# A fused decoder layer: new hand-written step orders for four engines, and a table of 281 identity products emptied

## What is computed

```python
def step(Sst, inp):                       # part 1: gated delta rule, 16 heads of 16
    qt, kt, vt, bt, gt = inp
    Sd = gt[..., None, None] * Sst
    kS = jnp.einsum('bhk,bhkv->bhv', kt, Sd)
    Snew = Sd + jnp.einsum('bhk,bhv->bhkv', kt, bt[..., None] * (vt - kS))
    ot = jnp.einsum('bhk,bhkv->bhv', qt, Snew)
    return (Snew, ot)
...
attn = a1 - lam * a2                      # part 2: two softmax attentions over 64 context tokens
...
ye = jax.nn.silu(jnp.einsum('bsd,eod->bseo', x1, expert_w) + expert_b)   # part 3: 8 experts,
combined = jnp.einsum('bse,bseo->bso', rw, ye)                           # two of them weighted per token
```

## Time and profile before

| | |
|---|---|
| median of 3 runs | 1671.31 us (1670.07 to 1680.73) |
| the profiled execution | 1671.47 us |
| its span | 1669.7 us |
| mean granted TensorE clock | 0.965 |
| TensorE, matmul busy | 1515.5 us, 91% of the span |
| VectorE busy | 1215.3 us, 73% |
| ScalarE busy | 858.9 us, 51% |
| GpSimd busy | 205.8 us, 12% |

### The profile page before, as it was taken

The page is one execution under the profiler, slowest core; times in us unless marked ns, Lnnn a source line. Parts: engine busy times, 40 slices in busy tenths (PEclk is TensorE's granted clock), DMA queues, the critical chain, the costliest instruction groups (busy, mean ns, idle before and its releaser), DMA issues.

```text
span 1669.7 us, 38572 instructions
## 1 busy us (share of the span) xinstructions
PE 1515.5 (91%) x16038; PEld 1013.4 (61%) x16090; DVE 1215.3 (73%) x3201; ACT 858.9 (51%) x1620; POOL 205.8 (12%) x212
## 2 busy tenths in 40 slices
...
DMA packets 20214, 31.69 MB, mean 19 GB/s; under 512 B 1480, under 2 KB 17864, under 8 KB 19784
## 3 DMA queue, kind: packets, MB, share of 16 engines
...
...
## 4 chain that ended last, share of the span: by engine, by line
PE 74%; DVE 17%; ACT 6%; issue 3%; DVEq 0%; ACTq 0%
PE bank L1766 11%; PE bank L1505 8%; PE bank L1714 7%; PE bank L1392 5%; PE four L1575 4%; PE bank L1704 4%; PE bank L1690 4%; PE bank L1507 3%; PE bank L1417 3%; DVE cs L1340 3%; PE four L1594 2%; PE four L1643 2%; PE bank L1432 2%; PE four L1417 2%; PE four L1627 2%
## 5 line engine op out<-in xcount | busy, mean ns | idle before, releaser
L1766 PE MATMUL bank<-w_sb,cs 128*128 128x512 f32 x512 | 260.2, 615 | 1.5 <-ACT cs L786 0.3
L786 ACT ACTIVATE cs<-bank 128x512 f32<-128x512 f32 x128 | 76.3, 596 | 235.0 <-remote 141.6
L505 POOL TENSOR_TENSOR decayed<-state,pk 128x512 f32<-128x512 f32 x64 | 70.7, 1105 | 825.1 <-DVE state L1160 825.1
L740 ACT COPY cs<-bank 128x512 f32<-128x512 f32 x128 | 74.9, 585 | 158.2 <-PE bank L1704 158.2
L1714 PE MATMUL bank<-vx_sb,cs 128*128 128x136 f32 x1024 | 141.3, 293 | 10.1 <-ACT cs L740 10.1
L1714 PEld LDWEIGHTS bank<-vx_sb,cs 128*128 128x128 f32 x1024 | 132.7, 199 | 22.3 <-ACT cs L740 14.6
L1505 PE MATMUL bank<-hT,w_sb 128*128 128x512 f32 x256 | 134.2, 649 | 9.9 <-ACT pre L590 6.8
L1766 PEld LDWEIGHTS bank<-w_sb,cs 128*128 128x128 f32 x512 | 90.0, 190 | 69.0 <-issue 60.1
L1340 DVE SCALAR_TENSOR_TENSOR cs<-cs,rwt 128x256 f32<-128x256 f32 x224 | 113.1, 505 | 24.7 <-ACT cs L786 13.0
L1704 PE MATMUL bank<-c_sb,cs 128*128 128x128 f32 x512 | 86.4, 294 | 30.7 <-ACT cs L740 16.1
L1238 DVE TENSOR_TENSOR cs<-bank,pkc 128x512 f32<-128x512 f32 x128 | 82.0, 682 | 30.6 <-PE bank L1704 30.6
...
## 6 DMA issues: line engine op xcount, KB each, us to landing
...
```

Of the source, the lines that this page charges most:

```text
L1766: mm(dst, x1T[:, k, b * TB:b * TB + TB], ew[:, k, ep * 512:ep * 512 + 512], start=k == 0, stop=False)
```

## The change

The lists of all four engines are replaced, the table KEEP is emptied, and `keep` (which then issues nothing) looks up another event to wait for. All steps stay, and each engine still runs each step once per turn. The core of the diff:

```diff
 ORDER = {
     "pe": steps('''
-        sum.0 sum.1 decay sum.2 +turn1.0 +turn1.1 -turn2.0 grow -turn2.1 -qx.0 sum.3 -sc.0.0 -qx.1 -sc.0.1 vturn raw.0
+        sum.0 sum.1 decay sum.2 +turn1.0 -turn2.0 +turn1.1 grow -turn2.1 -qx.0 sum.3 -sc.0.0 -qx.1 -sc.0.1 vturn raw.0
...
     "act": steps('''
...
-        -turn5.1 -turn6.0 -hnorm.1 -ffd.0 -turn6.1 osq.1 onorm.0 onorm.1 -ffd.1 +silu.2'''),
...
+        -turn5.1 -turn6.0 -hnorm.1 -ffd.0 -turn6.1 osq.1 onorm.0 onorm.1 -ffd.1'''),
     "pool": steps('''
         spread kx.0 kx.1 kx.2 kx.3 scale.0 kx.4 scale.1 kx.5 kx.6 scale.2 kx.7 scale.3 scale.4 scale.5 scale.6 scale.7
-        dec.0 dec.1 dec.2 dec.3 dec.4 dec.5 dec.6 -ffd.0 dec.7 -ffd.1 +bv'''),
+        dec.0 dec.1 dec.2 dec.3 dec.4 dec.5 +bv dec.6 -ffd.0 dec.7 -ffd.1'''),
...
-KEEP = {(-1, -1, "moe", 20): 3, (-1, -1, "moe", 25): 17, (-1, -1, "moe", 31): 1, (-1, -1, "moe", 7): 8, (-1, -1, "pt",
...
+KEEP = {}
...
+            emptied = [None]
+
             def keep(i, count):
 
                 if count and i > 0:
-                    pe.wait_ge(ev["pre_sb"].sem, ev["pre_sb"].at(min(i, NI - 1), 8))
+                    name, *at = emptied[0]
+                    pe.wait_ge(ev[name].sem, ev[name].at(*at))
                 for _ in range(count):
                     mm(bank[7 if i > 0 else 6][:, 0:P], ident, ident, start=True, stop=True)
```

More of the change, by code:

```diff
@@ L116 @@
     "pe": steps('''
-        sum.0 sum.1 decay sum.2 +turn1.0 +turn1.1 -turn2.0 grow -turn2.1 -qx.0 sum.3 -sc.0.0 -qx.1 -sc.0.1 vturn raw.0
+        sum.0 sum.1 decay sum.2 +turn1.0 -turn2.0 +turn1.1 grow -turn2.1 -qx.0 sum.3 -sc.0.0 -qx.1 -sc.0.1 vturn raw.0
         -sc.1.0 -sc.1.1 -pt.0 raw.1 -pt.1 raw.2 -pv.0 raw.3 -sc.2.0 -sc.2.1 -pt.2 raw.4 -pt.3 raw.5 -pv.1 -sc.3.0
-        -sc.3.1 raw.6 -pt.4 +rot.0 -pt.5 raw.7 -pv.2 +rot.1 -sc.4.0 -sc.4.1 -pt.6 +gate.0 -pt.7 d1.0 -pv.3 -sc.5.0
-        -sc.5.1 +unrot -pt.8 -pt.9 +gate.1 -pv.4 -sc.6.0 -sc.6.1 -pt.10 +cond -pt.11 -pv.5 -sc.7.0 -sc.7.1 -pt.12 +db
@@ L121 @@
[L121 to L125, removed]
@@ L126 @@
-        co.4.0 -moe.22 co.4.1 cs.5.0 -moe.23 cs.5.1 co.5.0 -moe.24 -moe.25 -moe.26 d1.6 co.5.1 -moe.27 -moe.28 -moe.29
-        -moe.30 -moe.31 cs.6.0 cs.6.1 -mi co.6.0 d1.7 co.6.1 -turn5.1 cs.7.0 -turn6.0 -mo.1 cs.7.1 co.7.0 co.7.1
-        -ffd.0 -turn6.1 onorm.0 onorm.1 wo.0 -ffu.0 -ffd.1 -ffu.1 wo.1'''),
-    "dve": steps('''
[L130 to L139, removed]
@@ L140 @@
-    "act": steps('''
[L141 to L148, removed]
-        -turn5.1 -turn6.0 -hnorm.1 -ffd.0 -turn6.1 osq.1 onorm.0 onorm.1 -ffd.1 +silu.2'''),
+        -sc.3.1 raw.6 -pt.4 +rot.0 -pt.5 raw.7 -pv.2 +rot.1 -sc.4.0 -sc.4.1 -pt.6 +gate.0 -pt.7 d1.0 -pv.3 +unrot
@@ new lines @@
+        -sc.5.0 -sc.5.1 -pt.8 -pt.9 +gate.1 -pv.4 -sc.6.0 -sc.6.1 -pt.10 +cond -pt.11 -pv.5 -sc.7.0 -sc.7.1 -pt.12
+        -pt.13 +db -pv.6 +proj.0 -turn3.0 -pt.14 +proj.1 -pt.15 -wp.0 z.0 -pv.7 +proj.2 -turn4.0 z.1 cs.0.0 +proj.3
+        -turn3.1 cs.0.1 z.2 -wp.1 +proj.4 z.3 d1.1 -pw.0 +proj.5 co.0.0 -turn4.1 co.0.1 cs.1.0 -router.0 cs.1.1 -moe.0
+        z.4 d1.2 +proj.6 co.1.0 -moe.1 co.1.1 cs.2.0 -pw.1 cs.2.1 +proj.7 -moe.2 z.5 d1.3 -moe.3 co.2.0 -router.1
+        co.2.1 cs.3.0 -moe.4 cs.3.1 -moe.5 z.6 d1.4 -moe.6 -moe.7 co.3.0 -moe.8 co.3.1 cs.4.0 -moe.9 cs.4.1 -moe.10
```

41 lines of the change are left out of this document (31 added, 10 removed).

## The result

The changed kernel took 1712.64 us (median of 4 runs, 1702.99 to 1716.57) where the kernel before took 1670.69 us. The ratio is 1.0231, with a 95% interval of 1.0171 to 1.0291. It is slower by 2.3%, clear of no change though not clear of 2%, and above the range that was forecast. The profiled execution took 1711.38 us, with a span of 1709.6 us and a mean granted clock of 0.92 where before had 0.965.

What follows compares the result with a forecast made beforehand. A steady turn was taken as bound by TensorE's work, with short waits. 1671.47 - 10 (steady order) - 1 (turn 7) - 6 (overruns) + 14 (lost clock) = 1668.5, stated as 1668 us; range 1648 to 1697, the forecast's own 1658 to 1680.

Steps and rivals of the forecast that it cites:

- The clock in turns 7 and 8: Half clock after removing identity products: +4 in turn 8 (one attention round 3.2, the end 1), no term for turn 7.
- The order in the steady turns: Turns 1 to 6: the new step order gives -1.7 us per turn, between +0.5 and -3.0; -10 for six.
- I take the half clock as staying, -0.3: Steady turn, pt.12 to proj.2: proj.0 still at half clock behind db, so -0.3 us; far end -1.57.
- unrot: Steady turn, moved ahead of sc.5: fills a TensorE wait for ScalarE, -0.6 us, bounds 0 and -0.77.
- The 1.05 before pt.14: Steady turn: TensorE's 1.05 us wait for VectorE behind pv.6 goes, since pv.6 now comes ahead of proj.0.
- the 0.77 ahead of pt.13: Steady turn: new 0.77 us wait for ScalarE's copy, because pt.13 now stands directly behind pt.12.
- co's halves apart: Steady turn: co.0 to co.3 split around an expert step, as co.4 was; -0.8 us, bounds 0 and -1.2.
- silu.2: ScalarE, moved from the turn's end to behind turn5.0: 0 us, at the far end +1 per turn.
- The clock in the head: Half clock without identity products: about +3 us in turn -1 (rot.0 and proj.0) and +7 in turn 0.
- rival A: Clock stays low wherever nothing feeds TensorE, in turns -1, 0 and 8: cost +43, total 1697.5 us, chance 0.17.
- The overruns that come back, -6: Turns 0, 7 and 8: identity products that ran past their waits no longer delay real work, -6 us.
- The argument against A: Turn 8: eight identity products ran at some 0.24 us a record, so feeding TensorE alone did not keep the clock up.

Runs made afterwards that it cites:

- The run with full clock: Changed kernel with all identity products put back, plus products in the steady-turn waits ahead of pt.13, ffu.1 and sum.0: 1647.40 us.
- the fastest version: Changed kernel with all identity products back, three steady-turn waits filled, and more products in turns 7 and 8: 1637.74 us.
- the run with the order of before: Kernel before with its step order kept and its table of identity products emptied: 1705.83 us, ratio 1.0207.

## Why the prediction was wrong

Two terms make up most of the 43 us between forecast and result. The clock in turns 7 and 8 was priced at nothing and at +4, and these turns lost 11.7 and 17.3 us. The half clock of the steady turns was taken as staying, and it grew, which took away some 7 of the 8 us that the order gives. For all the identity products the forecast had 14 - 6 = 8 us, and putting them back gave 37.6.

**The order in the steady turns: the size was right, the clock term was not.** Take half of the time at 0.50 off a turn's length. The six turns of before then give 183.7 to 184.1 us, whatever they show (185.8 us with 3.4 of half clock, 187.5 with 6.8, 189.2 with 10.2, 190.6 with 13.7), and those of after 187.8 - 10.2 / 2 = 182.7. The run with full clock measured 182.8, so this reckoning holds. The order gives 1.4 us per turn, and -1.7 was forecast. The step that failed is "I take the half clock as staying, -0.3" in the stretch from pt.12 to proj.2. The half clock didn't stay as it was: behind db it became 6.8 us in every turn, where before had 3.4 in three turns and 6.8 in the other three, and 3.4 at the end of every turn. Over six turns that is 61.4 us instead of 47.7, some 7 us of the 8 that the order gives. From pt.12 to proj.2 the row was to move by -0.3, and in the turn compared (one of 3.4 before) it moved by +1.5: 696.25 - 675.17 = 21.1 against 19.6.

By its parts: unrot gave its 0.6 us (pt.9 stands 0.60 earlier in the turn). The 1.05 before pt.14 went and the 0.77 ahead of pt.13 came, as worked out, and that small wait turned out to matter for the clock: with products in it the stretch behind db was gone in all six turns of three profiled runs, and in three of the six turns of the fastest version. co's halves apart gave about 0.6 of the 0.8. silu.2 gave 0, as said: the 2.29 us ahead of sum.0 stand unchanged. ffu.1 waits 2.62 instead of 2.19 us, with ffu.0 ahead of onorm.0 now. VectorE's wait stayed, as shown.

**The clock in the head: the size about right, the places not.** Turn -1 lost 4.4 us, against +3, and turn 0 7.8, against about +4. TensorE's timeline of the kernel after shows the places: rot.0, rot.1 and proj.0 of turn -1.

```profile
20.74 3.78 PE L1382 MATMUL bank<-hT,w_sb 128*128 128x512 f32 x4 [2.28 <-DVE hT L966]
29.65 3.78 PE L1382 MATMUL bank<-hT,w_sb 128*128 128x512 f32 x4 [5.13 <-DVE rota L977]
...
51.17 3.42 PE L1503 MATMUL bank<-hT,w_sb 128*128 128x512 f32 x4 [0.32 <-DVE edb L1036]
```

The forecast had rot.0 and proj.0, at 1.3 each. rot.0 cost nothing, because rot.1 waited for VectorE anyway and started at 29.65 us where before had 29.64. proj.0 cost 1.4 us. rot.1 cost 1.8 and the products of db 1.6, and neither was in the forecast, so that its +3 came near 4.4 by luck. The other projections ran at full clock, so rival A's price for turn -1 (10) was too high.

**The clock in the tail: the term that failed most.** Turn 7 had no clock term at all in the forecast, and turn 8 had "one of the four rounds", +4. Measured were +11.7 and +17.3 us. In the kernel after four of the six rounds between the first pv of turn 8 and its seventh take 9.6 us, as in the window shown, and the other two 8.3 us; the late rounds of turn 7 do the same. In turn 7 the products account for 7.7 of the 11.7 us (the run with the order of before), and the new order without them for the other 4.0. Rival A had the mechanism, but priced turn 8 at 17.8 us, turn 7 at nothing and the steady turns at a gain of 10. With +11.7 for turn 7 and -1.3 for the steady turns it would have been near 1718 us.

**The overruns that come back, -6: one seen, the sum open.** VectorE's wait behind co.6 in turn 0 fell from 2.59 us to 0.92 us, 1.7 of the 1.8 us that were forecast there, while the work ahead ran slower. For the other places no run tells the overrun from the clock.

```profile
215.81 0.48 DVE L1143 SCALAR_TENSOR_TENSOR rq<-four,c_sb,vT 128x256 f32<-128x256 f32 x1 [0.92 <-PE four L1611]
```

**The argument against A was misread.** That eight products ran at 0.24 us a record didn't show that feeding doesn't work. With more of them in the same rounds the clock was 0.99. The Trainium skill, "TensorE: Matmul & The Clock Gate", section "Part 1: The HAM clock gate", says that the throttled clock is the default and that activity releases it. The prediction weighed this and set it aside in part. Turn 8 agrees with it: its clock was 0.73 without products, 0.88 with those of before and 0.99 with more.

Two of the prediction's sums are off by 0.1 us (two places at 0.4 come to 0.8, eight projections at 1.29 to 10.3), which moves nothing.

Not tried: single entries of the table of products, and the place around db with VectorE's list changed to match. How much of turn 0's loss belongs to which step stays open. The products alone account for 7.3 us of it in the order of before, and for 4.6 in the new one.
